# The prologue's loads of a four-layer kernel in the order of their use, with a count for each group

## The reference

```
# layer 0 (layer 1 has the same modulation, layers 2 and 3 one with scale and shift only)
ada = silu(c) @ Wada.T + bada;  shift, scale, gate = split(ada, 3)
x_ssm = ln(ln(x) * (1 + scale) + shift)
mz = x_ssm @ Wz.T + bz
z1 = ssm(mz @ Wc1.T + bc1);  z2 = flip(ssm(flip(mz @ Wc2.T + bc2)))
out = (silu(x_ssm @ Wx.T + bx) * (z1 + z2)) @ Wf.T + bf + skip
x = x + gate * out
# layer 1 works on h[:, itok] and writes back with y[:, itok]
```

## Time and profile before

| | |
|---|---|
| median of 3 runs | 3895.41 us (3886.71 to 3902.54) |
| the profiled execution, its own time | 3887.06 us |
| its span in the trace | 3885.3 us |
| mean granted TensorE clock | 0.938 |
| PE busy | 3405.1 us, 88% |
| POOL, ACT, DVE busy | 2859.1, 2898.8, 2839.1 us (74%, 75%, 73%) |
| read from HBM | 233.16 MB, 61 GB/s over the span |

### The profile page before, as it was taken

The page is one execution under the profiler, slowest core; times in us unless marked ns, Lnnn a source line. Parts: engine busy times, 40 slices in busy tenths (PEclk is TensorE's granted clock), DMA queues, the critical chain, the costliest instruction groups (busy, mean ns, idle before and its releaser), DMA issues. The chain is left out here.

```text
span 3885.3 us, 66431 instructions
## 1 busy us (share of the span) xinstructions
PE 3405.1 (88%) x22974; PEld 2923.2 (75%) x22974; DVE 2839.1 (73%) x3589; ACT 2898.8 (75%) x6592; POOL 2859.1 (74%) x3087
## 2 busy tenths in 40 slices
PE   4677788999999998999999998999999899898876
PEld 2466677888888787888878787878878787876655
DVE  0468788787887878787887878787878878773421
ACT  1668788788888888888888788888888788854422
POOL 0478999888887888788888888887888878861400
PEclk9799999999999999999999999999999999997766
DMA  4112222222122212222221212222222212210100
GB/s 163 49 54 80 79 71 79 66 65 78 59 85 59 80 61 79 63 66 78 60 83 59 82 61 80 62 73 69 66 78 61 83 58 73 63 54 18 39 7 3
DMA packets 140814, 257.19 MB, mean 66 GB/s; under 512 B 15905, under 2 KB 33313, under 8 KB 140081
## 3 DMA queue, kind: packets, MB, share of 16 engines
q1 hardware_dynamic: 140482, 252.95, 21.2%
HBM read 233.16 MB, written 5.05 MB: 61 GB/s over the span
## 5 line engine op out<-in xcount | busy, mean ns | idle before, releaser
L682 POOL TENSOR_TENSOR g<-hst,c_bc 128x512 f32<-128x512 f32 x1536 | 1978.3, 1288 | 569.4 <-PE ps_y L591 415.9
L667 DVE TENSOR_TENSOR_SCAN hst<-decay,ps_b 128x512 f32<-128x512 f32 x1536 | 1835.6, 1211 | 509.6 <-PE ps_b L563 244.4
L628 ACT ACTIVATE decay<-delta,acoef 128x256 f32<-128x256 f32 x3072 | 1376.9, 498 | 11.4 <-DVE hst L667 11.0
L563 PE MATMUL ps_b<-ident,dbut 128*128 128x128 f32 x6144 | 964.7, 281 | 267.0 <-DVE hst L667 151.8
L647 POOL TENSOR_TENSOR dbut<-dut,bcm 128x256 f32<-128x256 f32 x1536 | 982.8, 640 | 217.9 <-ACT dut L853 217.9
L563 PEld LDWEIGHTS ps_b<-ident,dbut 128*128 128x128 f32 x6144 | 724.9, 145 | 347.0 <-issue 234.7
L591 PE MATMUL ps_y<-ident,g 128*128 128x128 f32 x6144 | 959.6, 280 | 14.7 <-issue 7.3
L591 PEld LDWEIGHTS ps_y<-ident,g 128*128 128x128 f32 x6144 | 760.5, 145 | 119.3 <-issue 35.2
L638 ACT ACTIVATE dbut<-dut,bcm 128x256 f32<-128x256 f32 x1536 | 767.1, 500 | 53.7 <-PE ps_b L563 50.3
L1303 PEld LDWEIGHTS ps_x<-v,pT 128*128 128x128 f32 x2048 | 276.6, 213 | 31.9 <-issue 28.0
L1303 PE MATMUL ps_x<-v,pT 128*128 128x17 f32 x2048 | 282.6, 277 | 3.2 <-ACT pT L1339 2.3
(11 more groups left out here) (188 smaller groups left out, 4092.1 us busy)
## 6 DMA issues: line engine op xcount, KB each, us to landing
c_bc<-c_rows SPq DMA_DIRECT2D x768, 256.0 KB, 3.2
rows_bc<-mod_rows SPq DMA_DIRECT2D x16, 384.0 KB, 4.4
weights<-in_weights_dram SPq DMA_DIRECT2D x1, 5792.0 KB
ada_w<-in_ada_w_dram SPq DMA_DIRECT2D x1, 5120.0 KB
x<-in_x_dram SPq DMA_DIRECT2D x16, 256.0 KB, 3.8
x0p<-x SPq DMA_DIRECT2D x16, 256.0 KB, 2.5
xr<-x SPq DMA_DIRECT2D x16, 256.0 KB, 3.6
x<-x SPq DMA_DIRECT2D x16, 256.0 KB, 3.6
```

Of the source, the lines that this page charges most:

```text
L563: last = nc.tensor.matmul(ps_b[:, u % 2, e * T + t * P:e * T + (t + 1) * P], dbut[:, u % NDBU, t, e * P:(e + 1) * P], ident[:, :], is_tran ...
L628: last = nc.scalar.activation(decay[:, u % (DA_AHEAD + 2), e, :], delta[s][:, eb, :], ACT.Exp, scale=acoef[:, s, eb, n:n + 1])
L667: nc.vector.tensor_tensor_scan(line(hst[:, u % NHST, :, :].rearrange("p e t -> p (e t)")), line(decay[:, u % (DA_AHEAD + 2), :, :].rearran ...
L682: nc.gpsimd.tensor_tensor(g[:, u % NG, :, :], hst[:, u % NHST, :, :], c_bc[:, k % NCB * CHUNK + n % CHUNK, :].unsqueeze(1) .broadcast_to([ ...
```

## The change

- WEIGHTS is put in another order: wdbc0, wdbc1 and wx come first, then wf and the rest. What lies ahead of `wf` (1920 of 11584 columns) is loaded by one transfer, what lies behind by another.
- The loads are issued in four groups: `ada` (condition, bias, modulation weights, norms' rows), `fold` (wz, wc, columns), `rest` (index vector, wdt_bias, first part of W), and the second part of W. Each has its own semaphore.
- ACT and PE begin with a wait for the `ada` group. PE waits for `fold` ahead of the fold, ACT ahead of the exponentials, DVE ahead of the folded biases.
- DVE's one-hot matrix stands behind the making of `rows`, with a wait for `rest`.
- The second part of W counts up a semaphore of the main part, `weights_in`, that the barrier between the parts does not clear. PE waits for it once, ahead of the first product with `wf` in `l0_post` of batch 0.

```diff
-WEIGHTS = dict(wx=(DB, E), wf=(EB, D), wdbc0=(EB, DBC), wdbc1=(EB, DBC),
+WEIGHTS = dict(wdbc0=(EB, DBC), wdbc1=(EB, DBC), wx=(DB, E), wf=(EB, D),
...
-                loads = [(W[:, :], dram["weights"]), (CO[:, :], dram["columns"]),
-                         (wdt_bias[:, :], dram["wdt_bias"]),
-                         (ada_w[:, :, :], dram["ada_w"]), (ada_b[:, :], dram["ada_b"]),
-                         (cond[:, :, :], dram["cond"]),
-                         (norm_rows[:, :, :], dram["norm_rows"].partition_broadcast(B)),
-                         (wz[:, :, :], dram["wz"]), (wc[:, :, :, :], dram["wc"]),
-                         (itok_i[:, :], dram["itok"].partition_broadcast(P))]
-                ALL_LOADED = 16 * len(loads)
+                early = WOFF["wf"][0]
+                ada = [(cond[:, :, :], dram["cond"]), (ada_b[:, :], dram["ada_b"]),
+                       (ada_w[:, :, :], dram["ada_w"]),
+                       (norm_rows[:, :, :], dram["norm_rows"].partition_broadcast(B))]
+                fold = [(wz[:, :, :], dram["wz"]), (wc[:, :, :, :], dram["wc"]), (CO[:, :], dram["columns"])]
+                rest = [(itok_i[:, :], dram["itok"].partition_broadcast(P)), (wdt_bias[:, :], dram["wdt_bias"]),
+                        (W[:, 0:early], dram["weights"][:, 0:early])]
+                ADA_LOADED, FOLD_LOADED, REST_LOADED = 16 * len(ada), 16 * len(fold), 16 * len(rest)
...
-                    for dst, src in loads:
-                        sp.dma_start(dst, src).then_inc(S["loaded"], 16)
+                    for dst, src in ada:
+                        sp.dma_start(dst, src).then_inc(S["loaded_ada"], 16)
+                    for dst, src in fold:
+                        sp.dma_start(dst, src).then_inc(S["loaded_fold"], 16)
+                    for dst, src in rest:
+                        sp.dma_start(dst, src).then_inc(S["loaded_rest"], 16)
+                    sp.dma_start(W[:, early:WTOT], dram["weights"][:, early:WTOT]).then_inc(stage_sems["weights_in"], 16)
...
-                    act.wait_ge(S["loaded"], ALL_LOADED)
+                    act.wait_ge(S["loaded_ada"], ADA_LOADED)
...
+                    act.wait_ge(S["loaded_fold"], FOLD_LOADED)
                     for s, a in enumerate((c["alog0"], c["alog1"], c["alog2"])):
...
-                    pe.wait_ge(S["loaded"], ALL_LOADED)
+                    pe.wait_ge(S["loaded_ada"], ADA_LOADED)
...
+                            pe.wait_ge(S["loaded_fold"], FOLD_LOADED)
                             pe.wait_ge(S["ada_taken"], NADA // 512)
...
+            if b == 0:
+                pe.wait_ge(S["weights_in"], 16)
             for t in range(TB):
                 to_tokens(pair[:, t, :], yg, t, w["wf"], 0, 2, EB, "bf")
```

More of the change, by code:

```diff
@@ L78 @@
 FIRST = """
-loaded consts cond_act ada_full ada_taken rows_ready rows_stored cols_full cols_taken alog_exp alog_done
+loaded_ada loaded_fold loaded_rest consts cond_act ada_full ada_taken rows_ready rows_stored cols_full cols_taken alog_exp alog_done
 fold_full fold_taken foldb_full foldb_done gather_ready dve_chain pool_chain
@@ L93 @@
 v3_sb q_sub q_exp k_sub k_exp qt_full qt_sb kt_full kt_sb bd_full bd_sb y3_full yn_3 yt_full_3 yt_sb_3
-h_full_3 res_3 out_done
+h_full_3 res_3 out_done weights_in
 """.split()
@@ L188, in build @@
         all_sems = range(sem_nums[0], sem_nums[-1] + 1)
+        stage_only = range(sem_nums[0], sem_nums[-1])
         mod_rows = nc.dram_tensor("mod_rows", (B, 4 * D), F32, kind="Internal").ap()
@@ L357, in done @@
                         dve.wait_ge(S["dve_chain"], n)
-                    dve.wait_ge(S["loaded"], ALL_LOADED)
                     dve.wait_ge(S["consts"], 1)
[L361 to L365, removed]
+                    dve.wait_ge(S["loaded_ada"], ADA_LOADED)
                     dve.wait_ge(S["ada_taken"], NADA // 512)
@@ L386, in _ @@
                     nc.vector.engine_nop().then_inc(S["rows_ready"], 1)
+                    dve.wait_ge(S["loaded_rest"], REST_LOADED)
+                    done(nc.vector.tensor_copy(itok[:, :], itok_i[:, :]))
+                    for k in range(TB):
+                        nc.vector.tensor_scalar(gath[:, k, :], itok[:, :], token[:, k:k + 1], None,
+                                                ALU.is_equal).then_inc(S["gather_ready"], 1)
+                    dve.wait_ge(S["loaded_fold"], FOLD_LOADED)
                     dve.wait_ge(S["foldb_full"], 1)
@@ L401, in _ @@
                     dve.wait_ge(S["fold_taken"], 4)
-            nc.multi_engine_barrier(list(mybir.ALL_ENGINES), sems_to_clear=all_sems)
+            nc.multi_engine_barrier(list(mybir.ALL_ENGINES), sems_to_clear=stage_only)
         S = stage_sems
```

## The result

The changed kernel takes 3872.11 us in the median of 20 runs (3849.66 to 3883.27), the kernel before 3888.7 us in the median of 20 (3873.91 to 3908.11). The ratio is 0.9948, with a 95% interval of 0.9935 to 0.996. The ratio stands for some 20 us; the two medians lie 16.6 us apart, and single runs of one kernel scatter over 34 us. The forecast was 3872.8 us. Seven more runs of the same kernel beside twelve of the kernel before gave 0.9928 (0.9902 to 0.9955). The profiled execution took 3865.97 us with a span of 3864.1 us, 21.2 us less than the span before.

A forecast was written before the change was run, and what follows sets the result against it. The prediction took the prologue to be bound by one wait for all ten loads, until 39.89 us. Loading the ada group first gains 22.6 us, all else costing nothing: 3895.41 - 22.6 = 3872.8 us, range 3858 to 3888.

The forecast's parts named there:

- The way of the argument: Prologue: work waits for all ten loads until 39.89 us; each microsecond sooner at the first product moves the whole program.
- The main term: Start of the prologue: with the ada group loaded first, ACT starts at 17.3 us instead of 39.89, gaining 22.6 us.
- the whole row of the first transfers of before: Loading of weights and columns in the kernel before: 6.10 MB in 16.0 us, 2.62 us per MB, used for the group.
- The bounds of this term: Ada group's loading: gain 24.1 us at 427 GB/s, 19.6 us at the 315 GB/s of small rows.
- The Trainium skill's share: Ada group's loading at about 358 GB/s per core: 15.1 us, gain 21.7 us; an estimate the sum does not use.
- The covers: Later loads and moved work behind the first group: all ready before use, cost nothing; fold group has 18 us cover.
- Products beside full transfers: Modulation products beside 400 GB/s transfers: no loss taken, bounded by 2.4 us of 24.04.
- The rival of transfers that share evenly: Prologue loads: ada_w complete only at 39 to 40 us, gain 0 to 2 us, 3894 us; chance 0.05.
- The rival of a part given back in the first batch: First batch: 11 us of PE work falls to the lower clock, gain 11.6 us, 3883.8 us; chance 0.07.
- The slower rival: First product through first batch's preparation: lower clock held, +46 us against -22.6, 3918.8 us; chance 0.03.
- Against the median: Whole time: 22.6 us taken off the three runs' median 3895.41 gives 3872.8 us, 0.58% less.
- The chances: Whole time: forecast 0.85; against the 0.5% bound, faster 0.63, same 0.34, slower 0.03.

The follow-up runs named there:

- the series: Changed kernel, fold group issued first, second part of W first, old order with counts kept, kernel before: silu at 18.68, 24.17, 29.15, 33.21, 39.89 us.
- the kernel with five pieces: Against the changed kernel, ada_w loaded in five transfers with own semaphores, norm_rows moved to the fold group: 3849.42 us against 3866.54.
- awaited late part: Against the changed kernel, DVE also waits in the prologue, behind rows, for the second part of the weights: 3862.97 us in one execution.
- the matrix at the head: Against the changed kernel, DVE's one-hot matrix and its wait for rest moved back ahead of the ada wait: 3867.98 us in one execution.

## Why the prediction was right, step by step

- **The way of the argument held.** One wait for all loads bounds the first 40 us, the prologue behind it is a line, and a start sooner by so much is an end sooner by so much: 21.2 us at the silu, 21.1 at the load of x, 21.6 at the first use of `wf`, 21.2 at the end of the first pair of profiles. The last of these four is partly luck, since single whole times scatter by more than that; the ratio over 20 runs each, some 20 us, carries it.
- **The main term was a little too large: 22.6 forecast, 21.2 measured.** The term that was mis-sized is the duration of the group: 14.2 us by 2.62 us per MB, where the silu at 18.68 leaves 15.6 (18.68 less the 0.4 behind the last data and the start at 2.7). The forecast scaled the whole row of the first transfers of before (16.0 us for 6.10 MB) with the bytes. By the 2.20 us per MB of the series only 1.5 us of it go with the 0.68 MB of difference, which gives 14.5: 0.3 us of the miss. The other 1.1 lie in the end of the group. In the DMA view of the kernel before, stretch 15.5:16, the last row of `weights` (46 KB) starts, and its share of the 16 engines' 0.5 us makes 1.7 us:

```profile
DMA packets 1, 0.05 MB, mean 93 GB/s; under 512 B 0, under 2 KB 0, under 8 KB 0
...
q1 hardware_dynamic: 1, 0.05, 21.4%
```

  In the changed kernel, stretch 14.6:15.4, the last row of `ada_w` (40 KB) starts, at 15.2, and takes 2.4 us (18.4% of 16 engines' 0.8 us):

```profile
DMA packets 1, 0.04 MB, mean 51 GB/s; under 512 B 0, under 2 KB 0, under 8 KB 0
...
q1 hardware_dynamic: 1, 0.04, 18.4%
```

  In the stretch behind it, 15.4:17.5, 96 of 111 packets are already rows of `wz` and semaphore writes; the other 15 fit 15 of the 16 rows of `norm_rows` (8 KB each):

```profile
DMA packets 111, 0.39 MB, mean 187 GB/s; under 512 B 30, under 2 KB 30, under 8 KB 96
```

  One packet of that size follows in 17.5:17.6, when the row of 2.4 us has ended:

```profile
DMA packets 9, 0.04 MB, mean 369 GB/s; under 512 B 1, under 2 KB 1, under 8 KB 8
```

  So the rows fit this: most engines are through with the group while one is not, and the count waits for it. The view does not name the engines. From the start of the last large row to the silu it is 3.5 us here; the forecast's row had 2.2 us from there to its last packets, and 0.4 more. The small loads have a part in the difference: with `norm_rows` out of the group and `ada_b` behind `ada_w` the silu came 0.5 to 0.8 us sooner. The rest is not taken apart.
- **The bounds of this term** (19.6 to 24.1) held the 21.2, and the silu's (15.8 to 20.3) held in every profile that issues the change's loads unedited.
- **The Trainium skill's share** (HBM Reference, table at the head) gave 21.7 as an estimate, by chance the nearest number. The trace does not show its 358 GB/s as a limit here, and goes with the page's addition that a core streaming alone measures above it: in 7:32 of the kernel with five pieces the windows view shows 426.

```profile
7.00:32.00 25.00, 24.19 (x50) 4.17 (x50) 0.00 (x0) 2.92 (x5) 0.00 (x0) 1.00 1.07 426
```

- **The covers all held.** Fold group in at 24.9 (foretold 24.2), rest at 30.0 (29.2), second part of W at 41.4 (41), first use at 257.3 (256). The awaited late part and the matrix at the head were tried, and no cost of their own showed. The store of `mod_rows` met the tail of W only in the kernel with five pieces, where it landed 3.4 us behind its issue at 37.75 (1.9 us in the changed kernel), still 17 us ahead of the load of x.
- **Products beside full transfers** cost nothing: 24.03 us against 24.04.
- **The rival of transfers that share evenly** is refuted by the series of five kernels. **The rival of a part given back in the first batch** asked for 11 us lost in the batch, behind the load of x. There the change brings 21.3 to 22.1 us at the first use of `wf`, profile against profile, so nothing is given back. A variation of this kind is real, though: 3.2 us from silu to load of x and 5 us from there to `wf` come and go in both kernels. **The slower rival** did not occur: products are fast after the first piece in every profile.
- **Against the median.** That the forecast 3872.8 and the measured 3872.11 agree within 0.7 us is luck. The three runs shown had a median of 3895.41, the 20 runs 3888.7. The base was 6.7 us too high and the gain 1.4 us too large; the two together would put the kernel at 3867.5, and that the median came out 4.6 us above this is within the scatter of the runs.
- **The chances** turned on 0.5%, beyond which a change can be told from none. Measured are 0.52%, with an interval of 0.40 to 0.65%: clear of no change, and on the edge of that bound, as the forecast of 0.58% with its 0.63 to 0.34 had it.

## What to carry to other kernels

The loads of one issuer arrived in the order of issue in every profile here, so what stands first in the list should be what the first instruction needs, and it needs a count of its own: order without counts gave nothing, counts without order a third of it. The same reasoning goes on into a large transfer: cut into pieces in the order of use, it let the first product start at 7.2 us where the group let it start at 19.1, and brought another 17 us in the medians, of which the profiles show 12. When the time to the first use of a group is estimated, not all of it goes with the bytes: at 2.2 us per MB some 3.7 us of the first group's 15.6 are left over (an estimate from the series), and a row from another kernel or another place has a remainder of its own, here 2.6 us.

## What the runs showed of the hardware that was not expected

- The stretch of one-column products runs 8.6 to 8.7 us or 10.5 to 11.6 us, in the same kernel, by the moment at which the granted clock falls in it, and its length goes with that of the first eight products, more than 30 us ahead of it. Three single profiles of one kernel differ by 3 us at the same landmark, and a landmark has to be compared with more than one profile.
- The scatter of the whole time goes with the mean granted clock of the execution. Over the 20 runs of the changed kernel the two correlate at -0.90, with 2.7 us less for each 0.001 of clock; over 14 runs of the kernel before, made beside the experiments, at -0.94 with 3.2 us. The lines stand at 3873.5 and 3893.6 us at a clock of 0.938, 20 us apart, and that of the five pieces (6 runs) at 3856.8. This is a correlation; no run set the clock, and why one execution is granted more than another stays open.
- ACT's table load fell behind the waits when four of them stood ahead of its first instruction, and added 1.28 us to the path.
